# One Perceiver layer: K projected before V in a step, V split at the step's end, and the chunk weights moved on VectorE

## The chip, the core and the metric

The kernel runs on one core of a Trainium2 chip. The metric is the device time of one execution in microseconds (us); lower is better.

## What is computed

A Perceiver layer on x (2 x 256 x 256) with a context (2 x 4096 x 256): cross-attention, self-attention, and a feed-forward part with quantized operands. Only the cross-attention matters here:

```python
q = (scale * (Q @ Wq + bq)).reshape(bs, q_len, NH, DM)      # 16 heads of 64
k = (K @ Wk + bk).reshape(bs, kv_len, NH, DM)               # K = V = ctx
v = (V @ Wv + bv).reshape(bs, kv_len, NH, DM)
qk = jnp.einsum('nlhd,nshd->nhls', q, k)
a = jax.nn.softmax(qk, axis=-1)
o = jnp.einsum('nhls,nshd->nlhd', a, v).reshape(bs, q_len, NH * DM)
return o @ Wo + bo
```

## The kernel before, in words

Each engine has its program written out by hand in one block of `cross_attention`; semaphores tie them. Every product of fp32 accuracy is made of three fp32r products: an operand is split into a high part (a rounded copy) and a low part (the rest). ScalarE makes the high part while it moves a result out of PSUM, VectorE the low part.

The work is cut into 8 groups (batch x four heads, `GP`), each into 16 steps (4 chunks of 1024 keys x 4 heads, `STEPS`), 128 steps in all. In step n, TensorE

1. makes the scores of step n+1 (`scores`, L295, into psS),
2. does a side job in the bank psW: `post` (L374, steps 0 to 7 of groups 1 to 7: turns the last group's outputs), `turn_o` (step 8), `project_o` (step 9), or `project_q` (L358, steps 12 to 15, the next group's queries),
3. turns the probabilities of step n (`turn`, L305) in four parts, with `values` (L318, probabilities times V) behind them,
4. between these, projects one piece of V (`project_v`, L346) and one piece of K (`project_k`, L333) for step n+4, both into psW,
5. in steps 0 to 7 of group 0 and in all of group 3, turns a piece of context at the step's end (`turn_ctx`, L369), again in psW.

psW is one bank, so each use waits until the one before has been moved out: V by ScalarE (`v_high`, L518) and VectorE (`v_low`, L618; semaphore `v_lo`), K by ScalarE alone (`k_raw`, L510; `kraw_ok`). `bank_free` (L440) is that wait at the start of a step. GpSimd splits K out of kraw (`split_piece`, L255) and, in step 11, the next group's weights (`split_w`, L232).

V lives in a ring of 7 buffers, which `v_high` guards:

```python
if m >= VRING:
    old = m - VRING
    wait(act, av_ok, 4 * (old // GH * GH + GH - 1) + old % GH + 1)
```

VectorE takes the row maxima of the scores (`maximum`, L606), which ScalarE's `exp` (L502) needs; it makes the low part of the queries (`q_low`, L623), of the probabilities (`p_low`, L612) and of V; in steps 0 to 7 it weighs the last group's outputs (`weigh_out`, L653, which frees psW, then `add_out`, L663). The weights of the four chunks of a group come from `weigh` (L635): six small instructions on 128 x 32 values, with an exponential by ScalarE (`edif`, L583) in their middle. Before the change they stand at the start of a group's last step.

The order within a step, before: on TensorE scores, side job, turn 0, turn 1, V, turn 2, values 0, turn 3, values 1, K, values 2, values 3.

Of the kernel before, what the change touches and what calls it, by code (L numbers as in the profile page):

```python
# [11 lines left out]
P = 128  # L12


def cross_attention(nc, x, ctx, Wq, bq, Wk, bk, Wv, bv, Wo, ident, y):
# [6 lines left out]
    QT = S // P  # L22
    CH = 1024
    NCH = CTX // CH
    PIECE = 512
    NP = CTX // PIECE
    GH = 4
# [5 lines left out]
    LEAD = 4  # L33
# [11 lines left out]
    with ExitStack() as st:  # L45
# [178 lines left out]
        @block.gpsimd  # L224
        def _(pool):
            pool.memset(ident[:, :], 0.0).then_inc(const_ok, 1)
            pool.memset(epst[:, :], EPS / SCALE ** 2).then_inc(const_ok, 1)
            pool.wait_ge(const_ok, 2)
            pool.affine_select(out=ident[:, :], in_=ident[:, :], compare_op=ALU.not_equal, fill=1.0, base=0,
                               pattern=[[-1, P]], channel_multiplier=1).then_inc(ident_ok, 1)  # L230

            def split_w(g, slot, w_s, raw, done):  # L232
                wait(pool, raw, 16 * (g + 1))
                src = wraw[:, slot, :, :]
                pool.tensor_copy(w_s[:, 0, :, :], src).then_inc(done, 1)
                wait(pool, done, 2 * g + 1)
                pool.tensor_tensor(w_s[:, 1, :, :], src, w_s[:, 0, :, :].bitcast(F32), ALU.subtract)\
                    .then_inc(done, 1)
                wait(pool, done, 2 * g + 2)

            def split_wq(g):
                wait(pool, raw_q, 16 * (g + 1))
                for twin in range(2):
                    for kt in range(KT):
                        src = wraw[:, 1, kt, :].rearrange("p (h d) -> p h d", h=GH)
                        pool.tensor_copy(wq_s[:, 0, kt, :, twin, :], src).then_inc(wq_ok, 1)
                wait(pool, wq_ok, 8 * g + 4)
                for twin in range(2):
                    for kt in range(KT):
                        src = wraw[:, 1, kt, :].rearrange("p (h d) -> p h d", h=GH)  # L250
                        pool.tensor_tensor(wq_s[:, 1, kt, :, twin, :], src, wq_s[:, 0, kt, :, twin, :].bitcast(F32),
                                           ALU.subtract).then_inc(wq_ok, 1)
                wait(pool, wq_ok, 8 * g + 8)

            def split_piece(m):  # L255
                wait(pool, kraw_ok, m + 1)
                raw = raw_of[m] if m < FIRST else kraw[:, :]
                pool.tensor_copy(khi[:, :], raw).then_inc(khi_ok, 1)  # L258
                wait(pool, khi_ok, m + 1)
                half = slice(HD * (m % 2), HD * (m % 2) + HD)  # L260
                for h in range(2):
                    own = slice(HD * h, HD * h + HD)
                    pool.tensor_copy(kT[half, m // 2 % KRING, h, 0, :], raw[own, :]).then_inc(k_split, 1)  # L263
                    pool.tensor_tensor(kT[half, m // 2 % KRING, h, 1, :], raw[own, :], khi[own, :].bitcast(F32),  # L264
                                       ALU.subtract).then_inc(k_split, 1)
                wait(pool, k_split, 4 * m + 4)

            split_w(0, 1, wk_s, raw_k, wk_ok)
            split_w(0, 0, wv_s, raw_v, wv_ok)
            split_piece(0)  # L270
            split_piece(1)
            split_wq(0)
            split_piece(2)
            split_piece(3)
            for n in range(N - LEAD):
                g, k = n // STEPS, n % STEPS
                if g + 1 < GP:
                    if k == 4:
                        wait(pool, q_ps, GH * (g + 1))
                        split_wq(g + 1)  # L280
                    if k == STEPS - LEAD - 1:
                        wait(pool, v_ps, n + LEAD + 1)
                        split_w(g + 1, 0, wv_s, raw_v, wv_ok)
                        wait(pool, k_ps, n + LEAD + 1)
                        split_w(g + 1, 1, wk_s, raw_k, wk_ok)
                split_piece(n + LEAD)

        @block.tensor
        def _(pe):
# [150 lines left out]
            def bank_free(n):  # L440

                if n == 0:
                    pe.wait_ge(q_ok, GH)
                elif prep_unit(n - 1) is not None:
                    wait(pe, prep_l, prep_unit(n - 1) + 1)
                else:
                    wait(pe, kraw_ok, min(n + LEAD, N))

            for n in range(N):
                g, k = n // STEPS, n % STEPS  # L450
                if n + 1 < N:
                    scores(n + 1)
                bank_free(n)
                if k < 8 and g >= 1:
                    post(g - 1, k, psW[:, :])
                elif k == 8 and g >= 1:
                    turn_o(g - 1)
                elif k == 9 and g >= 1:
                    project_o(g - 1)
                elif k >= 12 and g + 1 < GP:  # L460
                    project_q(g + 1, k - 12, psW[:, 0:S])
                turn(n, 0)
                turn(n, 1)
                if n + LEAD < N:
                    if k < 8 and g >= 1:
                        wait(pe, comb, 16 * (g - 1) + 2 * k + 1)
                    elif k == 8 and g >= 1:
                        wait(pe, o2_ok, 2 * g)
                    elif k == 9 and g >= 1:
                        wait(pe, y_ok, g)  # L470
                    elif k >= 12 and g + 1 < GP:
                        wait(pe, q_ok, GH * (g + 1) + k - 12 + 1)
                    project_v(n + LEAD, psW[:, :])
                turn(n, 2)
                values(n, 0)
                turn(n, 3)
                values(n, 1)
                if n + LEAD < N:
                    wait(pe, v_lo, n + LEAD + 1)
                    project_k(n + LEAD, psW[:, :])  # L480
                values(n, 2)
                values(n, 3)
                u = prep_unit(n)
                if u is not None:
                    wait(pe, cst_in, 16 * (u // KT - FIRST + 1))
                    wait(pe, kraw_ok, n + LEAD + 1)
                    turn_ctx(u, cst, psW[:, :])

            for k in range(8):
                dst = (psW[:, :], bank_S[0], bank_S[1], bank_S[2])[k % 4]  # L490
                if k == 0:
                    pe.wait_ge(kraw_ok, N)
                    pe.wait_ge(exp_ok, 2 * N)
                if k >= 4:
                    wait(pe, comb, 16 * (GP - 1) + 2 * (k - 4) + 1)
                post(GP - 1, k, dst)
# [4 lines left out]
        def _(act):  # L501
# [72 lines left out]
            for n in range(N):  # L574
# [3 lines left out]
                    o_out(g - 1)  # L578
                elif k >= 12 and g + 1 < GP:
                    q_high(g + 1, k - 12, psW[:, 0:S])  # L580
                if k == STEPS - 1:
                    wait(act, dif_ok, g + 1)
                    act.activation(edif[:, :, :, :], dif[:, :, :, :], ACT.Exp).then_inc(edif_ok, 1)  # L583
                p_high(n, 0)
                p_high(n, 1)
                if n + 1 < N:
                    exp(n + 1, 0)
                if n + LEAD < N:
                    v_high(n + LEAD, psW[:, :])
                p_high(n, 2)  # L590
                p_high(n, 3)
                if n + 1 < N:
                    exp(n + 1, 1)
                if n + LEAD < N:
                    k_raw(n + LEAD, psW[:, :])
                wait(act, av_ok, 4 * n + 4)
                if c == 1:
                    wait(act, post_ps, 8 * (g - 1) + 2 * h + 2)
# [6 lines left out]
        def _(dve):  # L605
# [26 lines left out]
                dve.tensor_tensor(ctxT_lo[:, half, keys], src, ctxT_hi[:, half, keys].bitcast(F32), ALU.subtract)\  # L632
                   .then_inc(prep_l, 1)

            def weigh(g):  # L635
                wide = lambda a: a[:, :].unsqueeze(2).to_broadcast([P, GH * QT, NCH])
                own = lambda a: flat4(a[:, g % 2, :, :, :])
                wait(dve, max_ok, 2 * STEPS * (g + 1))
                dve.tensor_reduce(negM[:, :], own(negm), AX.X, ALU.min).then_inc(negM_ok, 1)
                wait(dve, negM_ok, g + 1)  # L640
                dve.tensor_tensor(flat4(dif[:, :, :, :]), wide(negM), own(negm), ALU.subtract).then_inc(dif_ok, 1)
                wait(dve, edif_ok, g + 1)
                wait(dve, exp_ok, 2 * STEPS * (g + 1))
                dve.tensor_tensor(flat4(le[:, :, :, :]), flat4(edif[:, :, :, :]), own(lsum), ALU.mult).then_inc(le_ok, 1)
# [66 lines left out]
                maximum(0, qt)  # L711
            for n in range(N):
                g, k = n // STEPS, n % STEPS
                if k == STEPS - 1:
                    weigh(g)
                if n + 1 < N:
                    maximum(n + 1, 0)
                if k < 8 and g >= 1:
# [6 lines left out]
                p_low(n, 1)  # L725
                if n + 1 < N:
                    maximum(n + 1, 1)
                if n + LEAD < N:
                    v_low(n + LEAD, psW[:, :])
                p_low(n, 2)  # L730
                p_low(n, 3)
                if k < 8 and g >= 1:
                    add_out(g - 1, k)
                if prep_unit(n) is not None:
                    prep_low(prep_unit(n), psW[:, :])
            for k in range(8):
# [657 lines left out]
```

## Time and profile before

| | before |
|---|---|
| median of 3 runs | 1493.27 us (1492.13 to 1496.78) |
| the profiled execution, its own time | 1492.45 us |
| its span | 1489.6 us |
| TensorE busy | 1360.7 us, 91% |
| VectorE busy | 1009.1 us, 68% |
| ScalarE busy | 884.6 us, 59% |
| GpSimd busy | 620.7 us, 42% |
| mean granted TensorE clock | 0.962 |

The cross-attention's steps fill the span from about 48 to 1264 us. In the profile's rows, PE is TensorE's product, PEld its weight load, DVE VectorE, ACT ScalarE, POOL GpSimd. TensorE's ends are modelled, so its starts are the better marks.

### The profile page before, as it was taken

How to read it: one execution, taken by the hardware profiler on the slowest of the kernel's cores; microseconds unless marked ns; L12 is line 12 of the kernel's file. 1: busy time of each engine (PE TensorE's matmuls, PEld its weight loads, DVE VectorE, ACT ScalarE, POOL GpSimd, SP SyncE). 2: the span in 40 equal slices, each digit the busy share in tenths (PEclk: the TensorE clock that was granted, in tenths of full speed). 3: DMA queues.
4: the chain of work that ended last, by engine and by line, in shares of the span. 5: the costliest groups of instructions: out<-in, count | busy, mean ns of one | idle time of the engine just before them, and what ended most of it. 6: DMA issues, size and time to landing. Idle time of an engine off the chain costs nothing. (4 is left out here: it accounts for less than half of the span.)

```text
span 1489.6 us, 24781 instructions
## 1 busy us (share of the span) xinstructions
PE 1360.7 (91%) x9380; PEld 1157.6 (78%) x9380; DVE 1009.1 (68%) x1407; ACT 884.6 (59%) x1716; POOL 620.7 (42%) x749
## 2 busy tenths in 40 slices
PE   5999999999999999999998999999989998389867
PEld 5788888887888788878887888788878886257734
DVE  3666677666766677667766776677667766469766
ACT  2676656665666566656666666666666666146511
POOL 5355535453545354544553455445553441000000
PEclk9999999999999999999999999999999999589979
DMA  4010000000000010100000000000000000300000
GB/s 121 15 44 1 15 1 8 8 15 1 8 9 29 1 37 29 37 29 1 8 19 4 1 8 8 16 1 8 8 1 1 1 8 1 95 0 1 1 1 14
DMA packets 25940, 22.95 MB, mean 15 GB/s; under 512 B 5472, under 2 KB 25568, under 8 KB 25824
## 3 DMA queue, kind: packets, MB, share of 16 engines
q1 hardware_dynamic: 25824, 21.39, 4.9%
q8 instruction: 75, 1.23, 0.4%
q14 instruction: 41, 0.34, 0.1%
HBM read 20.86 MB, written 0.52 MB: 14 GB/s over the span
## 5 line engine op out<-in xcount | busy, mean ns | idle before, releaser
L609 DVE TENSOR_REDUCE negm<-psS 128x1 f32<-128x1024 f32 x256 | 312.0, 1219 | 183.0 <-PE psS L303 183.0
L540 ACT ACTIVATE pT_hi<-psT 128x512 fp32r<-128x512 f32 x512 | 290.0, 599 | 219.8 <-PE psT L313 218.0
L615 DVE TENSOR_TENSOR pT_lo<-psT,pT_hi 128x512 fp32r<-128x512 f32 x512 | 331.4, 684 | 53.4 <-ACT pT_hi L540 50.5
L264 POOL TENSOR_TENSOR kT<-kraw,khi 64x512 fp32r<-64x512 f32 x252 | 323.4, 1283 | 0.0
L258 POOL CAST khi<-kraw 128x512 fp32r<-128x512 f32 x126 | 77.1, 612 | 581.0 <-ACT kraw L516 580.1
L313 PE MATMUL psT<-ident,prob 128*128 128x128 f32 x2048 | 293.8, 277 | 4.2 <-DVE pT_lo L615 4.2
L506 ACT ACTIVATE prob<-psS,negm 128x1024 f32<-128x1024 f32 x256 | 286.5, 1119 | 15.2 <-DVE negm L609 15.2
L329 PE MATMUL psO<-pT_hi,v 128*128 128x256 f32 x1024 | 285.4, 306 | 1.1 <-DVE pT_lo L615 1.0
L330 PE MATMUL psO<-pT_lo,v 128*128 128x256 f32 x1024 | 262.6, 283 | 0.0
L313 PEld LDWEIGHTS psT<-ident,prob 128*128 128x128 f32 x2048 | 236.9, 142 | 16.5 <-issue 7.1
L329 PEld LDWEIGHTS psO<-pT_hi,v 128*128 128x128 f32 x1024 | 196.2, 192 | 7.3 <-DVE pT_lo L615 2.1
L330 PEld LDWEIGHTS psO<-pT_lo,v 128*128 128x128 f32 x1024 | 197.1, 192 | 5.2
L354 PE MATMUL psW<-wv_s,ctxT_hi 128*128 128x256 f32 x1000 | 175.6, 299 | 27.7 <-DVE q_lo L626 26.6
L303 PE MATMUL psS<-kT,q_hi 64*128 64x512 f32 x1024 | 195.2, 418 | 3.3 <-ACT prob L506 2.0
L354 PEld LDWEIGHTS psW<-wv_s,ctxT_hi 128*128 128x128 f32 x1000 | 138.7, 194 | 46.2 <-DVE q_lo L626 33.2
L263 POOL CAST kT<-kraw 64x512 fp32r<-64x512 f32 x252 | 153.8, 610 | 15.6
L341 PE MATMUL psW<-ctxT_hi,wk_s 128*128 128x512 f32 x496 | 144.8, 414 | 16.3 <-DVE v L620 15.3
L303 PEld LDWEIGHTS psS<-kT,q_hi 64*128 64x128 f32 x1024 | 96.2, 184 | 39.5 <-issue 6.4
L341 PEld LDWEIGHTS psW<-ctxT_hi,wk_s 128*128 128x128 f32 x496 | 83.7, 188 | 40.7 <-DVE v L620 26.4
L516 ACT ACTIVATE kraw<-psW,bkT 128x512 f32<-128x512 f32 x124 | 85.5, 689 | 40.2 <-PE psW L341 36.3
L620 DVE TENSOR_TENSOR v<-psW,v 128x512 fp32r<-128x512 f32 x125 | 85.7, 686 | 32.9 <-ACT v L523 32.9
L523 ACT ACTIVATE v<-psW 128x512 fp32r<-128x512 f32 x125 | 75.6, 605 | 46.7 <-PE psO L330 42.3
(213 smaller groups left out, 1630.7 us busy)
## 6 DMA issues: line engine op xcount, KB each, us to landing
cst<-in_ctx_dram SPq DMA_DIRECT2D x12, 512.0 KB, 3.8
oT<-in_ctx_dram SPq DMA_DIRECT2D x4, 512.0 KB, 5.0
wraw<-in_L_xattn_Wk_dram SPq DMA_DIRECT2D x8, 256.0 KB, 2.6
wraw<-in_L_xattn_Wv_dram SPq DMA_DIRECT2D x8, 256.0 KB, 3.9
wraw<-in_L_xattn_Wq_dram SPq DMA_DIRECT2D x8, 256.0 KB, 3.4
wo<-in_L_xattn_Wo_dram SPq DMA_DIRECT2D x8, 256.0 KB, 2.8
ff_wdn<-in_L_ffn_w_down_dram SPq DMA_DIRECT2D x1, 704.0 KB, 8.2
ff_win<-in_L_ffn_w_gate_dram SPq DMA_DIRECT2D x1, 640.0 KB, 5.8
```

The source lines that it names most:

```text
L263: pool.tensor_copy(kT[half, m // 2 % KRING, h, 0, :], raw[own, :]).then_inc(k_split, 1)
L264: pool.tensor_tensor(kT[half, m // 2 % KRING, h, 1, :], raw[own, :], khi[own, :].bitcast(F32), ALU.subtract).then_inc(k_split, 1)
L303: last = mm(psS[:, qt, half * PIECE:(half + 1) * PIECE], q[rows, h, qt * P:(qt + 1) * P], kT[rows, n // 2 % KRING, h % 2, part, :], start= ...
L313: last = pe.transpose(psT[:, t % 2, k * S + qt * P:k * S + qt * P + P], prob[:, prob_slot(n, qt), (2 * t + k) * P:(2 * t + k + 1) * P], id ...
L329: mm(psO[:, 0:S], w, pT_hi[:, at, k * S:(k + 1) * S], start=(t == 0 and k == 0), stop=False)
L330: last = mm(psO[:, 0:S], w, pT_lo[:, at, k * S:(k + 1) * S], start=False, stop=(t == TB - 1 and k == 1))
L341: last = mm(dst, wk_s[:, a, kt, i // 2 * P:(i // 2 + 1) * P], x_[:, kt, piece * PIECE:(piece + 1) * PIECE], start=(j == 0 and kt == 0), st ...
L354: last = mm(dst[:, k * GD:(k + 1) * GD], x_[:, kt, keys], wv_s[:, a, kt, :], start=(j == 0 and kt == 0), stop=(j == 2 and kt == KT - 1))
L506: act.activation(prob[:, prob_slot(n, qt), :], psS[:, qt, :], ACT.Exp, bias=negm[:, g % 2, h, qt, c:c + 1], accum_out=lsum[:, g % 2, h, qt ...
L540: act.activation(pT_hi[:, i % PRING, :], psT[:, t % 2, :], ACT.Copy).then_inc(ph_ok, 1)
L609: dve.tensor_reduce(negm[:, g % 2, h, qt, c:c + 1], psS[:, qt, :], AX.X, ALU.max, negate=True)\
L615: dve.tensor_tensor(pT_lo[:, i % PRING, :], psT[:, t % 2, :], pT_hi[:, i % PRING, :].bitcast(F32), ALU.subtract).then_inc(pl_ok, 1)
```

## The change

K is projected where V was and V where K was; TensorE, ScalarE and VectorE follow suit. V's two evictions now stand at the end of a step. `bank_free`, the wait before `turn_ctx` and the one before the last `post` become waits for `v_lo`. `weigh` is cut in two: `weigh_max` goes to the end of a group's step 14 on VectorE, `weigh_end` to the end of step 15, and ScalarE's `edif` two instructions later in step 15. On GpSimd the weights of K are split before those of V.

```diff
@@ gpsimd @@
                     if k == STEPS - LEAD - 1:
+                        wait(pool, k_ps, n + LEAD + 1)
+                        split_w(g + 1, 1, wk_s, raw_k, wk_ok)
                         wait(pool, v_ps, n + LEAD + 1)
                         split_w(g + 1, 0, wv_s, raw_v, wv_ok)
-                        wait(pool, k_ps, n + LEAD + 1)
-                        split_w(g + 1, 1, wk_s, raw_k, wk_ok)
@@ tensor @@
                 else:
-                    wait(pe, kraw_ok, min(n + LEAD, N))
+                    wait(pe, v_lo, min(n + LEAD, N))
...
-                    project_v(n + LEAD, psW[:, :])
+                    project_k(n + LEAD, psW[:, :])
                 turn(n, 2)
                 values(n, 0)
                 turn(n, 3)
                 values(n, 1)
                 if n + LEAD < N:
-                    wait(pe, v_lo, n + LEAD + 1)
-                    project_k(n + LEAD, psW[:, :])
+                    wait(pe, kraw_ok, n + LEAD + 1)
+                    project_v(n + LEAD, psW[:, :])
                 values(n, 2)
                 values(n, 3)
                 u = prep_unit(n)
                 if u is not None:
                     wait(pe, cst_in, 16 * (u // KT - FIRST + 1))
-                    wait(pe, kraw_ok, n + LEAD + 1)
+                    wait(pe, v_lo, n + LEAD + 1)
                     turn_ctx(u, cst, psW[:, :])
...
-                    pe.wait_ge(kraw_ok, N)
+                    pe.wait_ge(v_lo, N)
@@ scalar @@
+                p_high(n, 0)
+                p_high(n, 1)
                 if k == STEPS - 1:
                     wait(act, dif_ok, g + 1)
                     act.activation(edif[:, :, :, :], dif[:, :, :, :], ACT.Exp).then_inc(edif_ok, 1)
-                p_high(n, 0)
-                p_high(n, 1)
                 if n + 1 < N:
                     exp(n + 1, 0)
                 if n + LEAD < N:
-                    v_high(n + LEAD, psW[:, :])
+                    k_raw(n + LEAD, psW[:, :])
                 p_high(n, 2)
                 p_high(n, 3)
                 if n + 1 < N:
                     exp(n + 1, 1)
                 if n + LEAD < N:
-                    k_raw(n + LEAD, psW[:, :])
+                    v_high(n + LEAD, psW[:, :])
@@ vector @@
-            def weigh(g):
+            def weigh_max(g):
                 own = lambda a: flat4(a[:, g % 2, :, :, :])
                 wait(dve, max_ok, 2 * STEPS * (g + 1))
                 dve.tensor_reduce(negM[:, :], own(negm), AX.X, ALU.min).then_inc(negM_ok, 1)
                 wait(dve, negM_ok, g + 1)
                 dve.tensor_tensor(flat4(dif[:, :, :, :]), wide(negM), own(negm), ALU.subtract).then_inc(dif_ok, 1)
+
+            def weigh_end(g):
+                own = lambda a: flat4(a[:, g % 2, :, :, :])
                 wait(dve, edif_ok, g + 1)
...
-                if k == STEPS - 1:
-                    weigh(g)
                 if n + 1 < N:
                     maximum(n + 1, 0)
...
+                p_low(n, 2)
+                p_low(n, 3)
                 if n + LEAD < N:
                     v_low(n + LEAD, psW[:, :])
-                p_low(n, 2)
-                p_low(n, 3)
                 if k < 8 and g >= 1:
                     add_out(g - 1, k)
+                if k == STEPS - 2:
+                    weigh_max(g)
+                if k == STEPS - 1:
+                    weigh_end(g)
                 if prep_unit(n) is not None:
                     prep_low(prep_unit(n), psW[:, :])
```

VectorE in step 1 of group 1, from the first maximum to the reduction of the weighed outputs (`on`), before and then after:

```order
L609 TENSOR_REDUCE negm<-psS 128x1
L659 TENSOR_TENSOR oweighed<-psW,wts 128x512
L615 TENSOR_TENSOR pT_lo<-psT,pT_hi 128x512 x2
L609 TENSOR_REDUCE negm<-psS 128x1
L620 TENSOR_TENSOR v<-psW,v 128x8x64
L615 TENSOR_TENSOR pT_lo<-psT,pT_hi 128x512 x2
L668 TENSOR_REDUCE on<-oweighed 128x64
```

```order
L609 TENSOR_REDUCE negm<-psS 128x1
L663 TENSOR_TENSOR oweighed<-psW,wts 128x512
L615 TENSOR_TENSOR pT_lo<-psT,pT_hi 128x512 x2
L609 TENSOR_REDUCE negm<-psS 128x1
L615 TENSOR_TENSOR pT_lo<-psT,pT_hi 128x512 x2
L620 TENSOR_TENSOR v<-psW,v 128x8x64
L672 TENSOR_REDUCE on<-oweighed 128x64
```

V's low part has moved behind the last two low parts of the probabilities, so the reduction into `on` stands behind V.

VectorE at the end of group 0, from V's low part of step 14 to the maximum of step 15, before (the first row) and then after, from V's low part of step 14 to the weighing of the next group's step 0:

```order
L620 TENSOR_TENSOR v<-psW,v 128x8x64
L615 TENSOR_TENSOR pT_lo<-psT,pT_hi 128x512 x2
L639 TENSOR_REDUCE negM<-negm 128x8
L641 TENSOR_TENSOR dif<-negM,negm 128x32
L644 TENSOR_TENSOR le<-edif,lsum 128x32
L646 TENSOR_REDUCE L<-le 128x8
L648 RECIPROCAL rL<-L 128x8
L651 TENSOR_TENSOR wts<-edif,rL 128x32
L609 TENSOR_REDUCE negm<-psS 128x1
```

```order
L642 TENSOR_TENSOR dif<-negM,negm 128x32
L609 TENSOR_REDUCE negm<-psS 128x1
L626 SCALAR_TENSOR_TENSOR q_lo<-psW,bqT,q_hi 128x256
L615 TENSOR_TENSOR pT_lo<-psT,pT_hi 128x512 x2
L609 TENSOR_REDUCE negm<-psS 128x1
L615 TENSOR_TENSOR pT_lo<-psT,pT_hi 128x512 x2
L620 TENSOR_TENSOR v<-psW,v 128x8x64
L648 TENSOR_TENSOR le<-edif,lsum 128x32
L650 TENSOR_REDUCE L<-le 128x8
L652 RECIPROCAL rL<-L 128x8
L655 TENSOR_TENSOR wts<-edif,rL 128x32
L609 TENSOR_REDUCE negm<-psS 128x1
```

The four instructions from `le` to `wts` have moved past the whole of step 15, and stand now before the first maximum of the next group's step 0.

## Rows read from the trace of the kernel before

**Rows 1.** Windows over last steps of a group: length, engines' busy us, granted clock.
```profile
183.58:199.01 15.43, 12.13 (x70) 10.89 (x70) 7.57 (x12) 6.52 (x13) 4.32 (x6) 0.78 0.00 0
...
959.38:972.35 12.97, 9.50 (x71) 8.13 (x70) 7.17 (x12) 6.51 (x13) 4.35 (x6) 1.00 0.01 2
...
sum 103.37, PE 79.56 PEld 70.21 DVE 53.25 ACT 46.21 POOL 30.24; mean PE 11.37 PEld 10.03 DVE 7.61 ACT 6.60 POOL 4.32
```

**Rows 2.** Timeline of group 0's last step (S 183.58): start, duration, instruction; then `le` by tile.
```profile
186.73 1.26 POOL L264 TENSOR_TENSOR kT<-kraw,khi 64x512 fp32r<-64x512 f32 x1
186.80 1.24 DVE L644 TENSOR_TENSOR le<-edif,lsum 128x32 f32<-128x32 f32 x1 [4.26 <-ACT edif L583]
188.64 1.22 DVE L609 TENSOR_REDUCE negm<-psS 128x1 f32<-128x1024 f32 x1
190.31 1.22 PE L354 MATMUL psW<-wv_s,ctxT_hi 128*128 128x256 f32 x4 [3.30 <-DVE q_lo L626]
...
L644 DVE TENSOR_TENSOR le<-edif,lsum x8: 192/1242/1244, 186.8 to 1258.3; 128x32 f32<-128x32 f32 x8
```

**Rows 3.** Waits of the whole span: engine, line, what it waited for, us, times, longest.
```profile
ACT v L523 <- PE psO L330: 42.3, 31, 3.9
PEld psW L341 <- DVE v L620: 26.4, 50, 0.9
```

**Rows 4.** Windows over steps 3, 10, 11 and 13 of group 1.
```profile
225.84:235.48 9.64, 9.07 (x67) 7.79 (x67) 7.21 (x9) 5.92 (x11) 4.34 (x6) 1.00 0.01 2
291.53:300.04 8.51, 8.45 (x64) 7.32 (x64) 5.44 (x7) 5.92 (x11) 4.34 (x6) 1.00 0.00 0
300.04:309.08 9.04, 8.47 (x63) 7.32 (x63) 5.53 (x7) 5.93 (x11) 6.88 (x9) 1.00 0.01 3
318.50:327.90 9.40, 9.19 (x69) 8.04 (x68) 6.03 (x8) 6.47 (x12) 4.33 (x6) 1.00 0.01 2
```

**Rows 5.** Timeline of step 1 of group 5 (S 830.03, next S 838.98).
```profile
831.03 1.23 DVE L609 TENSOR_REDUCE negm<-psS 128x1 f32<-128x1024 f32 x1 [1.41 <-PE psS L303]
...
833.06 0.74 PE L354 MATMUL psW<-wv_s,ctxT_hi 128*128 128x256 f32 x4
...
836.45 1.19 PE L341 MATMUL psW<-ctxT_hi,wk_s 128*128 128x512 f32 x4
...
837.51 1.07 DVE L668 TENSOR_REDUCE on<-oweighed 128x64 f32<-128x512 f32 x1
...
838.98 0.50 PE L303 MATMUL psS<-kT,q_hi 64*128 64x512 f32 x2
```

**Rows 6.** Timeline of step 13 of group 5 (next S 949.98).
```profile
944.21 0.74 PE L354 MATMUL psW<-wv_s,ctxT_hi 128*128 128x256 f32 x4 [0.21 <-DVE q_lo L626]
...
945.95 0.60 ACT L523 ACTIVATE v<-psW 128x512 fp32r<-128x512 f32 x1 [0.17 <-PE psW L354]
...
946.58 0.69 DVE L620 TENSOR_TENSOR v<-psW,v 128x512 fp32r<-128x512 f32 x1
...
947.18 1.44 DVE L615 TENSOR_TENSOR pT_lo<-psT,pT_hi 128x512 fp32r<-128x512 f32 x2
...
947.57 1.08 PE L341 MATMUL psW<-ctxT_hi,wk_s 128*128 128x512 f32 x4
...
948.94 0.28 PE L329 MATMUL psO<-pT_hi,v 128*128 128x256 f32 x1
```

**Rows 7.** Timeline around a turn of context, group 3, steps 4 and 5.
```profile
554.30 0.63 PE L371 MATMUL psW<-ident,cst 128*128 128x128 f32 x4
...
554.86 0.50 PE L303 MATMUL psS<-kT,q_hi 64*128 64x512 f32 x2
...
556.21 1.22 DVE L609 TENSOR_REDUCE negm<-psS 128x1 f32<-128x1024 f32 x1
...
558.07 0.50 PE L354 MATMUL psW<-wv_s,ctxT_hi 128*128 128x256 f32 x2
```

More of the change, by code:

```diff
@@ L633, in prep_low @@
                    .then_inc(prep_l, 1)
-            def weigh(g):
-                wide = lambda a: a[:, :].unsqueeze(2).to_broadcast([P, GH * QT, NCH])
+            wide = lambda a: a[:, :].unsqueeze(2).to_broadcast([P, GH * QT, NCH])
+            def weigh_max(g):
                 own = lambda a: flat4(a[:, g % 2, :, :, :])
```

## The prediction, as put on record before the changed kernel ran

> **What bounds the kernel now.** I name steps by their place in a group, 0 to 15, and groups 0 to 7; S is the moment at which TensorE starts the score products of a step, and times inside a step count from it. The views were read in this order: windows cut at S, the waits, then the timeline of single steps.
>
> A usual step runs at TensorE's own pace: 8.95 us from S to S in a step of the first half (830.03 to 838.98, [rows 5]), 8.51 in step 10 [rows 4]. Three things break that. First, the last step of a group: seven of them take 103.37 us together [rows 1], 15.43 the first, where the step before takes 9.40 [rows 4]. The timeline shows why [rows 2]: `le` starts at +3.22, after 4.26 us in which VectorE waited for ScalarE's `edif`; the row maximum of the next step comes only at +5.06, `q_lo` after it, and the first projection, which waits for `q_lo`, at +6.73 behind 3.30 us of idle TensorE. The granted clock in that stretch is 0.78, so for part of it TensorE had 1.2 GHz and not 2.4, right behind that idle time; the one such step in which the clock stayed at 1.00 took 12.97 [rows 1]. Second, steps 3, 7 and 11: 9.64 against 8.95, 9.04 against 8.51 [rows 4, 5]. ScalarE's first half of V's split waits 31 times, 42.3 us, for a product of probabilities and V of the same step [rows 3]: the ring of seven V buffers. Third, TensorE waits 50 times, 26.4 us, for VectorE's second half of V's split before it may project K into psW [rows 3].
>
> **What the change moves.** Nothing is added or removed but the split of one ScalarE batch; instruction counts and transfers are the same. A step's length comes from four pieces. A is the start of the first projection. From the end of it to the natural start of the second lie 1.81 us of transposes and products: in step 13 of group 5, V starts at 944.21, K at 947.57, which is 3.36, less V's 1.55 [rows 6]. V's slot I take as 1.53, K's as 1.37 where TensorE had not to wait before it [rows 6], and from the next product to S it is 1.04 (948.94 to 949.98). Where TensorE had waited, K's slot is 838.98 - 1.04 - 836.45 = 1.49 [rows 5]. The length will be A + K + 1.81 + 1.53 + 1.04. Turned round, this gives A now: in step 13, 9.40 - 1.54 - 1.81 - 1.37 - 1.04 = 3.64 (3.65 below); in step 10, 8.51 less a wait of 0.2 before K, 2.44. That 0.2 is what is left of the 26.4 us [rows 3] when 31 ring waits of 0.7 are taken off: 4.7 over 19.
>
> When is psW free, and when VectorE? V now ends the step. From a V start, ScalarE's part begins at +1.74, VectorE's at +2.37, the next VectorE instruction at +2.97, and the part itself (0.69) is done at +3.06, or 3.12 with the signal [rows 6]. The next S is at V + 1.53 + 1.04 = V + 2.57. Three costs follow.
>
> *Weighted steps (0 to 7 of groups 1 to 7).* The reduction into `on` (1.07, [rows 5]) moves behind V's split. It ends, with the usual overlap of 0.09, at V + 3.95, which is S + 1.39; the maximum starts then, not at +1.00. From a maximum to the projection that waits for the weighing behind it is 1.86 (556.21 to 558.07, [rows 7]). So A becomes 3.25, where it is 3.03 now [rows 5]: length 3.25 + 1.49 + 1.81 + 1.53 + 1.04 = 9.12. Bounds: A unchanged (3.03), if the reduction overlaps more; 3.45 without any overlap.
>
> *Steps that end with a turn of context (0 to 7 of group 0, all of group 3).* The turn may write psW only when V's split is done: V + 3.12 instead of V + 2.57, a stall of 0.55, beside the 0.56 of the turn itself [rows 7]. Bounds 0.4 and 0.7. In the same steps the maximum is already at +1.35 [rows 7], so the reduction costs nothing more.
>
> *Step 0 after a group.* The four instructions `le`, `L`, `rL`, `wts` now stand between V's split and the next maximum. `le` lasted 1.24 while GpSimd had an instruction under way: it ended 0.05 after that one (186.73 + 1.26 = 187.99, [rows 2]); its shortest is 0.19 [rows 2]. From its end to the maximum 0.60 [rows 2]. With 0.7 for `le`, the maximum is at V + 2.97 + 1.3 = S + 1.7, A = 3.6, length 9.47. Bounds: `le` 0.19, A = 3.05; or `le` and `wts` both held for a full 1.26, A = 5.2. The Trainium skill (SBUF — State Buffer, Who interferes with whom) says that a VectorE instruction with two SBUF inputs contends with a GpSimd instruction that reads SBUF, whichever starts first keeping the ports for its whole length. The trace agrees: 1.24 against 0.19. By that rule the move is not free, since it puts both instructions where GpSimd still splits K; without it `le` would take 0.19 and the sum be 2.8 lower.
>
> What goes: the ring wait (V's eviction now comes after the product that it waits for) and the wait for V's split before the second projection. In its place TensorE waits there for ScalarE's `kraw` alone. If that starts as late behind K as V's eviction behind V, 1.74, and lasts 0.7, it is done at 2.5, and V's turn comes at 1.49 + 1.81 = 3.3. At step 14 the two instructions of `weigh_max` fit in before S + 1.00. The maximum of the last step is then free, and A is that of step 13, 3.65. On GpSimd K's weights come first and V's second; it is busy 6.88 of the 9.04 us of step 11, 4.33 of another [rows 4]. The K piece behind both comes later than now by the order alone, so `kraw` of step 12 may wait; the 0.8 of slack just worked out hides it. Uncovered, it would cost under 1 us in seven steps.
>
> **The sum, against the profiled execution (1492.45 us).**
> Last steps: 7 x 9.52 (3.65 + 1.49 + 1.81 + 1.53 + 1.04) + 1.1 in group 3 = 67.7, from 103.4: -35.6.
> Ring steps: 12 weighted ones 9.64 to 9.12, -6.2; step 11 of seven groups 9.04 to 8.19 (A = 2.44, K = 1.37), -6.0; five with a turn, which win the ring's 0.5 to 0.7 and lose 0.3 to 0.5, -1.2.
> Plain steps: 9 from 8.51 to 8.19, -2.9; step 8 of six groups, 0.2 each for the same wait, -1.2.
> Weighted steps without ring: 30 x (9.12 - 8.95) = +5.1; step 0: 5 x 0.5 = +2.5, after group 3 +0.1.
> Steps 12 to 14 of six groups: 9.40 to 9.52 (the slots 1.49 and 1.53, where they were 1.54 and 1.37): 18 x 0.12 = +2.2.
> Steps with a turn: six of group 0, +0.23 each (8.19 + 1.11 against 9.07); in group 3 eight of +0.67 (from the turn's 0.55 and the slot's 0.12), step 0 +1.1, steps 8 to 10 together +1.1: +8.9.
> Total -34.3, or 1458.1. The median of the runs shown, 1493.27, lies 0.8 above the profiled execution, inside what runs differ by. Forecast 1458. A measurement of this kernel can tell about 0.3%, 4.5 us, from no change.
>
> **Rivals.** *The weights are held by GpSimd.* Both two-input instructions wait for a full one: A = 5.2 in six steps, each 1.6 more than above, 9.6 in all: 1468. For it: five of eight `le` took the full time (median 1242 ns, [rows 2]). Against: GpSimd works 4.33 of 9.40 us [rows 4], so the second of two instructions that stand some 0.5 us apart finds it idle more often than not. Chance 0.08. The page of the Trainium skill named above would have it so if both were caught.
>
> *V's tail costs the full price.* The reduction and both evictions overlap less than I read: A = 3.45 in 42 steps (+8.4), the turn's stall 0.7 in 24 (+3.6): 1470. For it: the order at the end of the step has never run. Chance 0.10. The mirror case, A unchanged (-9.2), gives 1449, chance 0.07.
>
> *The last steps keep their hole.* If the first projection there were still late, say because `q_hi` and not the weights set it, the 35.6 stay: 1493, no change. Against: the projection started 1.67 behind the maximum [rows 2], as `q_lo` stands between them, and step 13 has the same `q_hi` with none of the weights. Chance 0.02.
>
> *Slower: psW becomes the chain.* Now maximum, `exp`, V's split, reduction and the next maximum form a ring over ScalarE and VectorE. V's split is done at S + 0.55. Half the scores are made by S + 1.00 [rows 5], so the side job behind them wants psW at some S + 1.6: 1.05 us of slack. If V's first half stood behind a late `exp` by more than that, every step would wait for it. The gain is gone when the 120 steps lose 0.3 us each, so from 1.3 us of lateness; at 1.5 it would be 120 x 0.46 = 55, 1513. Against: neither engine is full, 7.21 and 5.92 us busy in a step of 9.64 [rows 4]. Chance 0.04.
>
> **How the numbers follow.** The forecast has 0.69 with its own range, 1452 to 1464. Down to 1447 the mirror case is in, up to 1470 the two dearer ones. Faster: 0.69 + 0.08 + 0.10 + 0.07 = 0.94; same 0.02; slower 0.04.
>
> **What would show it.** In the changed profile: last steps of a group at 9.5 us and clock 1.00; no wait of ScalarE's V eviction for a product; weighted steps near 9.12 with the maximum at S + 1.4 and a short wait of K's projection for the weighing; a wait of 0.5 before each turn of context; step 10 at 8.2. I am wrong if weighted steps take over 9.3, if TensorE waits for V's split at the start of ordinary steps, or if the last steps stay above 11.

## The result, and the profile of the changed kernel

| | before | after |
|---|---|---|
| median of 4 runs each | 1493.58 us (1492.13 to 1496.78) | 1455.70 us (1455.16 to 1458.58) |
| profiled execution: time, span | 1492.45, 1489.6 us | 1458.58, 1456.7 us |
| steps 1 to 125, from S to S | 1194.07 us | 1155.67 us |

The ratio of the times is 0.9747 (95% interval 0.9727 to 0.9768): 37.9 us less. The forecast was 1458. The third line of the table is what the rest is measured by: the windows view over one stretch, from S of step 1 to S of step 126. What lies outside of it is hardly touched by the change, but differs from execution to execution: over the ten kernels profiled here the beginning takes 53.9 to 58.0 us and the end 239.3 to 243.1; after takes 1.7 us more at the beginning than before and 3.8 more at the end. So the stretch fell by 38.4 us, close to the 37.9 of the medians, and the span of this one execution by 32.9.

The page of the profile after: span, engines' busy time, granted clock in tenths in 40 slices, and the group of V's second half on VectorE.

```profile
span 1456.7 us, 24781 instructions
PE 1342.8 (92%) x9380; PEld 1140.1 (78%) x9380; DVE 1026.6 (70%) x1407; ACT 888.1 (61%) x1716; POOL 622.1 (43%) x749
PEclk9999999999999999999999999999999999679868
L620 DVE TENSOR_TENSOR v<-psW,v 128x512 fp32r<-128x512 f32 x125 | 86.5, 692 | 149.6 <-ACT v L523 149.6
```

VectorE now has 149.6 us of idle time ahead of V's second half, and some instructions are queued behind it that would have fitted in there. The experiments come back to this.

Windows cut at S: first three of the seven last steps of a group with the sum over all seven, which answer to [rows 1].

```profile
185.00:194.46 9.46, 9.24 (x69) 8.01 (x68) 6.83 (x11) 6.60 (x13) 4.33 (x6) 1.00 0.00 0
...
641.28:651.92 10.64, 9.88 (x74) 8.44 (x74) 7.54 (x11) 7.19 (x14) 4.32 (x5) 1.00 0.01 2
...
934.64:944.08 9.44, 9.23 (x69) 8.02 (x69) 7.12 (x11) 6.59 (x13) 4.63 (x7) 1.00 0.01 2
...
sum 67.33, PE 65.30 PEld 56.52 DVE 48.84 ACT 46.74 POOL 30.64; mean PE 9.33 PEld 8.07 DVE 6.98 ACT 6.68 POOL 4.38
```

They take 67.33 us where they took 103.37, and the granted clock is 1.00 in all seven. The same view over steps 2, 3, 10 and 13 of group 1, which answers to [rows 4]:

```profile
213.03:222.10 9.07, 8.93 (x67) 7.69 (x66) 7.22 (x10) 6.04 (x11) 4.33 (x6) 1.00 0.01 3
222.10:231.16 9.06, 8.92 (x67) 7.71 (x66) 7.22 (x10) 6.04 (x11) 4.35 (x6) 1.00 0.01 3
286.51:294.74 8.23, 8.23 (x65) 7.25 (x64) 5.64 (x8) 5.86 (x11) 4.18 (x5) 1.00 0.00 0
...
312.39:321.83 9.44, 9.23 (x69) 8.01 (x68) 6.20 (x9) 6.48 (x12) 4.85 (x7) 1.00 0.01 2
```

Step 3 is now as long as step 2 beside it (9.06, 9.07): the ring of V buffers costs nothing any more. Step 10 has TensorE busy for its whole length. The waits of the whole span, which answer to [rows 3]:

```profile
ACT v L523 <- PE psW L354: 26.3, 119, 0.7
...
PEld psW L341 <- DVE oweighed L663: 23.5, 56, 1.0
...
PE psW L371 <- DVE v L620: 13.2, 24, 0.6
```

ScalarE's V eviction waits for its own projection alone, at most 0.7 us; its 42.3 us for a product are gone. TensorE's 26.4 us for VectorE before K are gone too. Two small waits are in their place: 56 for the weighing before K, in the first half of a group, and 24 of 0.55 for V's second half before a turn of context.

Where the 38.4 us went, each class of steps summed from its windows (S to S):

| steps | before | after | difference | forecast |
|---|---|---|---|---|
| last of a group, 7 | 103.37 | 67.33 | -36.0 | -35.6 |
| 3, 7, 11 without a turn, 19 | 179.07 | 166.22 | -12.9 | -12.2 |
| 1, 2, 4, 5, 6 without a turn, 30 | 268.47 | 271.74 | +3.3 | +5.1 |
| 0 without a turn, 6 | 53.69 | 56.75 | +3.1 | +2.6 |
| 12 to 14 of six groups, 18 | 169.42 | 170.05 | +0.6 | +2.2 |
| steps with a turn, 22 | 211.68 | 220.08 | +8.4 | +7.7 |
| all others, 23 | 208.37 | 203.50 | -4.9 | -4.1 |
| steps 1 to 125 | 1194.07 | 1155.67 | -38.4 | -34.3 |

### The profile page after: what moved, and what is told of

It is laid out like the page before. It is cut to its first block and busy times, and to the rows that moved or that the text cites. A ratio compares the mean times of both kernels' runs of the same rounds, so it can differ in the third digit from the quotient of the medians.

```text
span 1456.7 us, 24781 instructions
## 1 busy us (share of the span) xinstructions
PE 1342.8 (92%) x9380; PEld 1140.1 (78%) x9380; DVE 1026.6 (70%) x1407; ACT 888.1 (61%) x1716; POOL 622.1 (43%) x749
## 5 line engine op out<-in xcount | busy, mean ns | idle before, releaser
L615 DVE TENSOR_TENSOR pT_lo<-psT,pT_hi 128x512 fp32r<-128x512 f32 x512 | 338.4, 688 | 95.2 <-ACT pT_hi L540 81.7
L313 PE MATMUL psT<-ident,prob 128*128 128x128 f32 x2048 | 288.7, 274 | 3.9 <-DVE pT_lo L615 3.9
L313 PEld LDWEIGHTS psT<-ident,prob 128*128 128x128 f32 x2048 | 237.2, 140 | 32.9 <-issue 7.1
L620 DVE TENSOR_TENSOR v<-psW,v 128x512 fp32r<-128x512 f32 x125 | 86.5, 692 | 149.6 <-ACT v L523 149.6
L341 PE MATMUL psW<-ctxT_hi,wk_s 128*128 128x512 f32 x496 | 148.2, 420 | 16.5 <-DVE q_lo L626 5.9
L354 PE MATMUL psW<-wv_s,ctxT_hi 128*128 128x256 f32 x1000 | 160.3, 282 | 0.0
L303 PE MATMUL psS<-kT,q_lo 64*128 64x512 f32 x512 | 101.4, 393 | 0.0
L354 PE MATMUL psW<-wv_s,ctxT_lo 128*128 128x256 f32 x500 | 100.7, 283 | 0.0
```

The costliest lines, as they stand in the source:

```text
L303: last = mm(psS[:, qt, half * PIECE:(half + 1) * PIECE], q[rows, h, qt * P:(qt + 1) * P], kT[rows, n // 2 % KRING, h % 2, part, :], start= ...
L313: last = pe.transpose(psT[:, t % 2, k * S + qt * P:k * S + qt * P + P], prob[:, prob_slot(n, qt), (2 * t + k) * P:(2 * t + k + 1) * P], id ...
L341: last = mm(dst, wk_s[:, a, kt, i // 2 * P:(i // 2 + 1) * P], x_[:, kt, piece * PIECE:(piece + 1) * PIECE], start=(j == 0 and kt == 0), st ...
L354: last = mm(dst[:, k * GD:(k + 1) * GD], x_[:, kt, keys], wv_s[:, a, kt, :], start=(j == 0 and kt == 0), stop=(j == 2 and kt == KT - 1))
L615: dve.tensor_tensor(pT_lo[:, i % PRING, :], psT[:, t % 2, :], pT_hi[:, i % PRING, :].bitcast(F32), ALU.subtract).then_inc(pl_ok, 1)
```

## The experiments

Each is compared with the kernel before, which ran beside it on the same chip: median 1493.99 us (1490.13 to 1494.98) for e1, e2, e3 and e5, 1490.83 us (1486.14 to 1495.30) for the others. Results first (ratio with its 95% interval, and steps 1 to 125 as above):

| run | median us | ratio | steps 1 to 125 |
|---|---|---|---|
| after | 1455.70 | 0.9747 (0.9727 to 0.9768) | 1155.67 |
| e1, weights alone | 1460.80 | 0.9787 (0.9766 to 0.9809) | 1162.82 |
| e2, K first alone | 1472.64 | 0.9857 (0.9842 to 0.9871) | 1173.36 |
| e8, no low half of one K piece | 1481.06 | 0.9934 (0.9910 to 0.9958) | 1183.65 |
| e3, reduction ahead of V | 1443.86 | 0.9664 (0.9649 to 0.9678) | 1146.06 |
| e5, weights ahead of V | 1449.55 | 0.9702 (0.9688 to 0.9717) | 1151.45 |
| e4, V first where a turn follows | 1445.32 | 0.9688 (0.9667 to 0.9710) | 1146.53 |
| e6a, e3 and e5 | 1440.14 | 0.9665 (0.9641 to 0.9690) | 1142.27 |
| e6, e3, e5 and e4 | 1432.22 | 0.9603 (0.9580 to 0.9625) | 1133.46 |

### e1: the weights moved, the projections as before

```diff
-                if k == STEPS - 1:
-                    weigh(g)
...
+                if k == STEPS - 2:
+                    weigh_max(g)
+                if k == STEPS - 1:
+                    weigh_end(g)
```

on VectorE, from the start of a step to its end, and on ScalarE `edif` behind the first two `p_high` calls, as in the change.

> The kernel before with the weights moved alone (V still projected first, K second). My theory: the hole in a group's last step goes, but step 15 keeps its V-ring wait: length 10.2 us in place of 13.0 to 15.4, granted clock 1.00 there, steps 3, 7, 11 unchanged at 9.65 and 9.05, step 0 unchanged at 8.95 (the weights run in VectorE's idle time). 1493.6 - 7 x 4.6 - 1.2 = about 1461. Rival, the hole is filled by another wait (q_hi): last steps stay above 13 us, 1485 or more. Rival, most of the whole gain comes from the order of K and V: 1480.

Measured 1460.80 us, 33.2 less than before. The windows over the last steps, first and sum:

```profile
183.11:193.38 10.27, 9.49 (x70) 8.12 (x69) 6.70 (x12) 6.47 (x13) 4.33 (x6) 1.00 0.00 0
...
sum 72.58, PE 66.87 PEld 57.17 DVE 47.46 ACT 45.91 POOL 30.26; mean PE 9.55 PEld 8.17 DVE 6.78 ACT 6.56 POOL 4.32
```

The hole is gone and the clock is 1.00; every other class of steps is within 0.3 us of the kernel before. What it takes over 9.44 is mostly the wait for a V buffer (K starts 0.73 us later than it does where nothing holds it), which the last step has as steps 3, 7 and 11 have it. This part of the change alone takes 31.3 us off steps 1 to 125, where both parts take off 38.4.

### e2: K first, the weights where they were

```diff
+                if k == STEPS - 1:
+                    weigh(g)
...
-                if k == STEPS - 2:
-                    weigh_max(g)
-                if k == STEPS - 1:
-                    weigh_end(g)
```

in the changed kernel: the whole weighing is back at the start of the last step, and `edif` ahead of `p_high(n, 0)`.

> The changed kernel with the six weight instructions and the exponential put back where they were. My theory: the holes stay (first projection of a last step at +6.7, clock below 1 in it, some 14.9 us), the ring waits go (steps 3, 7: 9.06; step 11: 8.22), weighted steps cost +0.11, turned steps +0.3 to +0.66: net -5.5 over ordinary steps and -3.5 in the last ones, 1484 to 1485. Rival, K first is worth nothing alone or loses, since the waits at the step's end eat it: 1493 or above. Rival, K first carries most of the gain: 1465.

Measured 1472.64 us: 12 less than expected, a miss. Windows over the last steps, three of them and the sum, then VectorE in the last step of group 0 (S 183.47) with TensorE's first projection, and `le` by tile:

```profile
183.47:196.53 13.06, 10.82 (x69) 9.25 (x68) 7.41 (x15) 6.73 (x13) 4.72 (x6) 0.87 0.00 0
...
481.82:493.31 11.49, 9.24 (x69) 8.04 (x68) 7.42 (x15) 6.62 (x13) 4.35 (x6) 1.00 0.00 1
...
1095.94:1107.44 11.50, 9.26 (x70) 8.02 (x70) 7.41 (x15) 6.62 (x13) 4.34 (x6) 1.00 0.00 1
sum 89.52, PE 73.27 PEld 63.45 DVE 52.44 ACT 47.48 POOL 34.06; mean PE 10.47 PEld 9.06 DVE 7.49 ACT 6.78 POOL 4.87
```

```profile
186.69 0.19 DVE L644 TENSOR_TENSOR le<-edif,lsum 128x32 f32<-128x32 f32 x1 [2.00 <-ACT edif L583]
...
187.49 1.22 DVE L609 TENSOR_REDUCE negm<-psS 128x1 f32<-128x1024 f32 x1
...
189.15 2.00 PE L341 MATMUL psW<-ctxT_hi,wk_s 128*128 128x512 f32 x4 [2.24 <-DVE q_lo L626]
...
L644 DVE TENSOR_TENSOR le<-edif,lsum x8: 191/191/192, 186.7 to 1237.8; 128x32 f32<-128x32 f32 x8
```

`le` still starts at S + 3.22, but lasts 0.19 in all eight cases, so the maximum comes at +4.02 instead of +5.06 and the first projection at +5.68. GpSimd has nothing under way there: since K is projected first, its pieces are split earlier in the step, and the second low half, which ran over `le` [rows 2], is over. I had left the hole at its old length. Over the seven steps the maximum comes 6.4 us earlier by this: 1.05 in five of them, but 0.51 in group 3 and 0.66 in group 5, where `le` had not been held for so long. Another 1.4 us of the miss lie in the ordinary steps, which fell by 6.9 us and not 5.5. The remaining 4 or so are in the last steps: the ring wait, which goes here too and is worth about 5 there (72.58 in e1, 67.33 with both parts) where I had 3.5 for the last steps in all, and the clock. The same 2.24 us of idle time cost clock in one step (0.87, 13.06 us) and not in another (1.00, 11.49 us).

The two parts alone take off 33.2 and 21.3 us, 54.5 together, and both at once 37.9 (in steps 1 to 125: 31.3 and 20.7, 52.0 together, and 38.4). They overlap: K first shortens the hole that the moved weights remove, and the moved weights pay in step 0 for GpSimd's low half only when K is projected first (steps 0: 53.75 in e1, 53.22 in e2, 56.75 with both).

### e8: `le` without GpSimd beside it

Was it GpSimd that held `le`, or did `le` wait for something else that K first moves too? In the kernel before, the two subtractions of one K piece of each group write 8 columns of 512, so most of that piece's low part is left out:

```diff
+                    cut = slice(0, 8 if m % STEPS == 2 and m >= STEPS else PIECE)
-                    pool.tensor_tensor(kT[half, m // 2 % KRING, h, 1, :], raw[own, :], khi[own, :].bitcast(F32),
+                    pool.tensor_tensor(kT[half, m // 2 % KRING, h, 1, cut], raw[own, cut], khi[own, cut].bitcast(F32),
```

> The kernel before; of the one K piece of each group that GpSimd splits during the hole, the two subtractions write 8 columns and not 512, so most of the low part of that piece of K is left out. My theory of le: it is held by GpSimd's instruction, so here it lasts 0.19 us in place of 1.24, the maximum comes at S + 4.0 in place of 5.06, and the first projection of the last step at 5.7 in place of 6.7: at least 7 us less than before, more if the TensorE clock falls less: 1480 to 1487. Rival, le is slow by itself after its wait (1.24 as before): 1493.

Measured 1481.06 us. Timeline of the last step of group 0 (S 181.16), and `le` by tile:

```profile
183.22 0.21 POOL L265 TENSOR_TENSOR kT<-kraw,khi 64x8 fp32r<-64x8 f32 x1
...
184.38 0.19 DVE L645 TENSOR_TENSOR le<-edif,lsum 128x32 f32<-128x32 f32 x1 [4.26 <-ACT edif L584]
...
185.18 1.22 DVE L610 TENSOR_REDUCE negm<-psS 128x1 f32<-128x1024 f32 x1
...
186.84 1.22 PE L355 MATMUL psW<-wv_s,ctxT_hi 128*128 128x256 f32 x4 [2.25 <-DVE q_lo L627]
...
L645 DVE TENSOR_TENSOR le<-edif,lsum x8: 191/192/194, 184.4 to 1245.5; 128x32 f32<-128x32 f32 x8
```

Only GpSimd's work was changed, and `le`, still starting at +3.22, fell from 1.24 to 0.19 us; maximum and projection stand at +4.02 and +5.68, as in e2. So the 1.05 us were GpSimd's, and they explain why K first alone shortens the hole. The last steps take 93.5 us instead of 103.4: 6.4 by the earlier maximum, as in e2, and the rest goes with the granted clock, which was 0.78 to 0.89 in six of the seven and 1.00 in one before, and is 0.87 or 0.88 in five and 1.00 in two here.

### e3: the reduction ahead of V's second half

```diff
-                if n + LEAD < N:
-                    v_low(n + LEAD, psW[:, :])
                 if k < 8 and g >= 1:
                     add_out(g - 1, k)
+                if n + LEAD < N:
+                    v_low(n + LEAD, psW[:, :])
```

in the changed kernel. If the +5 us of weighted steps come from the reduction behind V's split, this returns them.

> The changed kernel with the reduction of the weighed outputs put before V's low part on VectorE. My theory: VectorE idles there some 1.5 us for ScalarE's high part, so the reduction is free, the maximum returns from S + 1.38 to S + 1.00, K's projection from 3.25 to 3.03, weighted steps from 9.06 to 8.82: 42 x 0.24 = 10 us less than the changed kernel, 1445 to 1446. Rival, the reduction pushes V's low part back by its own length: weighted steps stay at 9.06 or grow, 1456 or more.

Measured 1443.86 us, 11.8 below after; in the steps 9.6 less. Windows over steps 1 to 6 of group 5, first of after, then of e3:

```profile
807.35:861.68 54.33, 53.51 (x397) 46.22 (x397) 43.32 (x55) 36.22 (x66) 30.33 (x39) 1.00 0.02 6
```

```profile
800.38:853.39 53.01, 53.01 (x398) 46.25 (x397) 44.43 (x55) 35.52 (x66) 30.25 (x39) 1.00 0.02 6
```

VectorE in step 1 of group 5, after (S 807.35, next 816.40), with TensorE's two projections:

```profile
807.14 0.69 DVE L620 TENSOR_TENSOR v<-psW,v 128x512 fp32r<-128x512 f32 x1 [1.22 <-ACT v L523]
...
807.74 1.07 DVE L672 TENSOR_REDUCE on<-oweighed 128x64 f32<-128x512 f32 x1
...
808.73 1.22 DVE L609 TENSOR_REDUCE negm<-psS 128x1 f32<-128x1024 f32 x1
...
810.60 1.20 PE L341 MATMUL psW<-ctxT_hi,wk_s 128*128 128x512 f32 x4
...
813.92 0.64 PE L354 MATMUL psW<-wv_s,ctxT_hi 128*128 128x256 f32 x4
```

VectorE idles 1.22 us ahead of V and then runs the reduction, so that the maximum comes 1.38 behind S and K 3.25 behind it. In e3, at the end of step 1 of group 4 (S of step 2 664.45):

```profile
662.92 1.08 DVE L672 TENSOR_REDUCE on<-oweighed 128x64 f32<-128x512 f32 x1
...
664.23 0.69 DVE L620 TENSOR_TENSOR v<-psW,v 128x512 fp32r<-128x512 f32 x1 [0.23 <-ACT v L523]
...
665.46 1.22 DVE L609 TENSOR_REDUCE negm<-psS 128x1 f32<-128x1024 f32 x1 [0.53 <-PE psS L303]
```

The reduction stands in that idle time, V is no later (0.22 ahead of the next S, 0.21 in after), and VectorE even waits 0.53 us for the scores. The maximum is at +1.01, K at +3.02, and TensorE is busy for all 53.01 us. The step is then 8.83, shorter than the 8.95 of the kernel before, which says that the order K, V is itself no dearer: all of the +3.3 of the table, and the 0.12 us a step that the order gains, had gone to the place of the reduction.

### e5: the weights ahead of V's second half

```diff
+                if k == STEPS - 1:
+                    weigh_end(g)
                 if n + LEAD < N:
                     v_low(n + LEAD, psW[:, :])
...
-                if k == STEPS - 1:
-                    weigh_end(g)
```

in the changed kernel.

> The changed kernel with the four last weight instructions put before V's low part in step 15. My theory: they too fit in the idle time before V's low part, the first maximum of step 0 returns from S + 1.84 to S + 1.00 and K's projection from 3.71 to 3.03, step 0 from 9.5 to 8.8: 6 x 0.7 = 4 us less, 1451 to 1452. If they meet GpSimd's instructions there, le lasts up to 1.24 us without cost. Rival, GpSimd holds them long enough to delay V's low part: no gain, 1455 to 1456.

Measured 1449.55 us, 6.2 below after, in the steps 4.2. After first, the end of group 4 (S of group 5's step 0 is 797.85), then e5 before step 0 of group 1 (S 192.84):

```profile
797.63 0.69 DVE L620 TENSOR_TENSOR v<-psW,v 128x512 fp32r<-128x512 f32 x1 [1.21 <-ACT v L523]
797.74 1.29 POOL L264 TENSOR_TENSOR kT<-kraw,khi 64x512 fp32r<-64x512 f32 x1
798.24 0.85 DVE L648 TENSOR_TENSOR le<-edif,lsum 128x32 f32<-128x32 f32 x1
...
799.58 0.19 DVE L655 TENSOR_TENSOR wts<-edif,rL 128x32 f32<-128x32 f32 x1
799.69 1.22 DVE L609 TENSOR_REDUCE negm<-psS 128x1 f32<-128x1024 f32 x1
```

```profile
191.32 0.82 DVE L648 TENSOR_TENSOR le<-edif,lsum 128x32 f32<-128x32 f32 x1
...
192.63 0.19 DVE L655 TENSOR_TENSOR wts<-edif,rL 128x32 f32<-128x32 f32 x1
192.74 0.69 DVE L620 TENSOR_TENSOR v<-psW,v 128x512 fp32r<-128x512 f32 x1
193.84 1.23 DVE L609 TENSOR_REDUCE negm<-psS 128x1 f32<-128x1024 f32 x1 [0.42 <-PE psS L303]
```

In after, `le` ends at 799.09, 0.06 behind GpSimd's instruction (797.74 + 1.29 = 799.03), and the maximum stands at S + 1.84. In e5 `le` is still long, but its length falls where VectorE was idle, and the maximum is at +1.00. Step 0 goes from 9.51 to 8.83.

### e4: V first in the steps that end with a turn of context

```diff
+        def v_first(n):
+            return prep_unit(n) is not None and n % 4 != 3
...
-                    project_k(n + LEAD, psW[:, :])
+                    (project_v if v_first(n) else project_k)(n + LEAD, psW[:, :])
...
-                    wait(pe, kraw_ok, n + LEAD + 1)
-                    project_v(n + LEAD, psW[:, :])
+                    wait(pe, v_lo if v_first(n) else kraw_ok, n + LEAD + 1)
+                    (project_k if v_first(n) else project_v)(n + LEAD, psW[:, :])
```

in the changed kernel, with the evictions on ScalarE and VectorE in the same order; in these steps the turn waits for `kraw_ok` and not for `v_lo`. Steps 3, 7, 11 and 15 keep K first, for the ring.

> The changed kernel, but in steps that end with a turn of context (and are not steps 3, 7, 11 or 15) V is again projected first and K second, so the turn waits for ScalarE's K eviction alone. My theory: the stall before those turns (0.6 us) goes, such steps return from 9.40 to 9.07 (group 0) and from 10.20 to 9.53 (group 3), 6 x 0.33 and 11 x 0.4 to 0.7: 8 to 9 us less than the changed kernel, 1447. Rival, the uneven spacing of K's pieces makes ScalarE wait for GpSimd where V first is followed by K first: under 4 us of gain.

Measured 1445.32 us; 9.1 less in the steps, of which 8.95 in those with a turn (220.08 to 211.13). Step 1 of group 3 and the turn behind it, after:

```profile
497.66:507.85 10.19, 9.55 (x71) 8.12 (x71) 7.86 (x11) 6.63 (x12) 4.34 (x5) 1.00 0.01 2
```

```profile
506.46 0.28 PE L330 MATMUL psO<-pT_lo,v 128*128 128x256 f32 x1
...
507.29 0.63 PE L371 MATMUL psW<-ident,cst 128*128 128x128 f32 x4 [0.55 <-DVE v L620]
```

The same step in e4:

```profile
493.22:502.75 9.53, 9.44 (x72) 8.15 (x72) 7.67 (x10) 6.63 (x12) 4.32 (x6) 1.00 0.01 2
```

The stall of 0.55 is gone and the step has its old length (9.53 in before too). By starts the stall was more than the row's idle time says: the turn starts 0.83 us behind the start of the last product in after, and 0.20 behind it in the kernel before (554.10 and 554.30, [rows 7]) and in e4, so it came 0.63 later. In these steps the new order had only cost; K needs psW for ScalarE's part alone, and V for VectorE's as well.

### e6a and e6: together

e6a is the edits of e3 and e5 in one kernel, with `add_out` and `weigh_end` ahead of V's second half.

> The changed kernel with both the reduction and the four weight instructions before V's low part. My theory: the two gains lie in different steps and add up, weighted steps 8.83 and step 0 8.83: 1493.6 - 50 - 6 = 1438 to 1439. Rival, they share one cause and do not add: 1444.

Measured 1440.14 us. In the steps it is 13.4 below after, where e3 and e5 alone gave 9.6 and 4.2, 13.8 together. Its ratio, 0.9665, is no better than e3's 0.9664; the two were measured beside different runs of the kernel before, whose medians lie 3.2 us apart, so by times alone the last 4 us are not shown, by the steps they are.

e6 has the edit of e4 as well.

> All three repairs together: reduction and weights before V's low part, V first in turning steps. If all are separate, 1438.5 - 8.5 = 1430. Rival, the repairs of group 3 overlap with the others: 1434 or more.

Measured 1432.22 us, ratio 0.9603: its interval lies wholly below that of the changed kernel, whose edits it extends. The steps fell by 22.2 us against after; the three edits alone gave 9.6, 4.2 and 9.1. They add up to within 0.8 us, and this version beats both kernels of the case.

## Why the prediction was right, and where its terms were off

**The hole in the last steps** was the whole case, and went as forecast: -36.0 against -35.6, steps of 9.44 for 9.52, 10.64 in group 3, clock 1.00. e1 shows that the moved weights do it alone. What I had not seen is that K first alone would take 13.8 of these us as well, 6.4 of them by way of GpSimd and about 5 with the ring wait; it did not matter for the sum, since there is only one hole to remove, but it is most of the 12 us by which the expectation of e2 was wrong.

**The ring wait and the wait before the second projection** are gone: -12.9 against -12.2. ScalarE waits for no product before V, and step 3 is as long as step 2.

**Weighted steps** were forecast at 9.12 with the maximum at S + 1.39 and the first projection at 3.25. Measured: 9.06, +1.37 or +1.38, 3.25. (By its own terms the prediction's maximum is at 3.95 - 2.57 = 1.38; the 1.39 is a slip.) The mechanism, the late reduction, is shown by e3.

**The slots of the two projections** were mis-sized. I took their lengths to belong to K and V: 1.49 (1.37 unwaited) and 1.53. They depend on the place too. V took 1.54 as the first projection and takes 1.44 as the second; K took 1.37 as the second, where nothing held it, and takes 1.48 to 1.52 as the first, in step 10 too, where TensorE waits for nothing. So the second place is about 0.1 shorter for both, and K about 0.05 shorter than V in either; why, no run here shows. In plain steps the two errors nearly cancel, K's 1.37 being 1.48 and V's 1.53 being 1.44 (step 10: 8.22 for 8.19); where I had taken 1.49 and 1.53, in weighted steps, ring steps, steps 12 to 14 and last steps, each came out 0.06 to 0.09 too long. That is most of the 4.1 us by which the sum was too small a gain. Another 0.7 is step 9 of six groups, which the sum left out and which went from 10.28 to 10.17.

**Step 0** was forecast at A = 3.6 from `le` at 0.7 and a maximum at S + 1.7. Measured: `le` 0.85 in the median, maximum +1.84, A 3.71, length 9.51 (9.71 in group 7, with the maximum at +2.03); +3.1 for +2.6. The rule of the Trainium skill (SBUF — State Buffer, Who interferes with whom) that made this term differ from nothing held, as e8 and the 0.06 us behind GpSimd's end show; without it the term would have been 2.8 lower by the prediction's own sum, and no run has `le` at 0.19 in that place. The rival in which `wts` was held too did not come: it took 0.19. It was nearer than its grounds said, though: in the kernel before, in group 5, `le` got off with 0.30 and `wts` was held to 0.74 (last section).

**Turned steps**: the stall was 0.55, as assumed (13.2 us over 24). Group 3's steps took 10.19 for 10.20; group 0's 9.40 for 9.30, the one place where the sum was too kind, +8.4 for +7.7. By starts the turn came 0.63 later and not 0.55 (e4), which is most of that 0.1. In group 3 the same error was there and was hidden by the opposite one in V's slot, so the hit at 10.19 is luck.

**The number.** The gain in the steps was 38.4 against 34.3. The profiled execution gave 5.5 of it back, 1.7 at its beginning and 3.8 at its end, where the page shows the clock at 6, 7, 9, 8, 6, 8 tenths in the last six slices (before: 5, 8, 9, 9, 7, 9; that the clock is the reason is not shown), so its 1458.58 meets the forecast of 1458 in part by chance; the median, 1455.7, is 2.3 below. None of the rivals came. The nearest to a live one, a slower chain over psW, would have shown as TensorE waiting at ordinary step starts, and TensorE is busy for all 8.23 us of step 10.

## What to carry to other kernels

Small late work on an in-order engine belongs in the idle time ahead of an instruction that has to wait, not behind it: here the same five instructions made the steps 13.4 us longer behind V's second half than ahead of it (e6a), where they delayed nothing, and the view that says so is the idle column of that one group. If two edits aim at one hole, measure each alone before adding their gains (33 and 21 us apart, 38 together). Swapping two operations for one engine's sake also moves when a third engine works, so ask of every such swap what now runs beside what; and use the swap only in the steps that need it (e4).

## What the runs showed of the hardware that was not expected

**A tiny VectorE instruction is held for the rest of a GpSimd one.** `le` reads two tiles of 128x32 from SBUF. It lasts 0.19 us alone (e2, e8: sixteen of sixteen) and up to 1.24 beside GpSimd's 64x512 subtraction, in the cases read until 0.05 or 0.06 after the end of that one. The group view showed it only as a median of 1242 ns beside a shortest of 192 [rows 2]; that spread was the sign. In the kernel before, the last step of group 5 shows more of it:

```profile
962.25 0.61 POOL L263 CAST kT<-kraw 64x512 fp32r<-64x512 f32 x1
962.60 0.30 DVE L644 TENSOR_TENSOR le<-edif,lsum 128x32 f32<-128x32 f32 x1 [4.26 <-ACT edif L583]
962.82 1.27 POOL L264 TENSOR_TENSOR kT<-kraw,khi 64x512 fp32r<-64x512 f32 x1
962.94 0.19 DVE L646 TENSOR_REDUCE L<-le 128x8 f32<-128x32 f32 x1
963.16 0.20 DVE L648 RECIPROCAL rL<-L 128x8 f32<-128x8 f32 x1
963.40 0.74 DVE L651 TENSOR_TENSOR wts<-edif,rL 128x32 f32<-128x32 f32 x1
```

`le` ends 0.04 us behind GpSimd's copy. `L` and `rL`, which read one tile each, then run in 0.19 and 0.20 while GpSimd's subtraction is under way, and `wts`, which reads two, takes 0.74 and ends 0.05 behind it (964.14, 964.09). So the instructions with two SBUF inputs were held, those with one were not.

**The granted clock does not follow from the hole alone.** In e2 the last steps all have the same 2.24 or 2.25 us of idle TensorE ahead of the first projection, but the row shows 0.87 in four of them and 0.88 in group 3, so part of the step at 1.2 GHz, and 1.00, all of it at 2.4 GHz, in two; the price is 13.06 - 11.49 = 1.6 us, by which TensorE's busy time grows as well (10.82, 9.24). In e1 and in after, where the hole is gone, it is 1.00 in all seven. A hole costs its own length, and in some of seven like steps this on top; which ones is not explained here. The step of the kernel before that kept 1.00 (12.97 us, [rows 1]) is the one of group 5 above, whose hole was shorter, 2.90 for 3.30, so it is not a measure of the clock's price alone.
